# Two chained depthwise convolutions with group norms on one core: pair transfers, windowed band tables, reordered engines, and one more crossed half taken by VectorE

## The chip, the cores and the metric

One core of a Trainium2 chip. The metric is the device time of one execution in microseconds, as a median over several runs; the profile is of one execution, and its span runs from the first to the last instruction.

## The reference

The input x has the shape 4 x 96 x 128 x 128 in float32. Cut to what matters:

```python
def _gn(v, G=32, eps=1e-05):          # mean and variance over 3 channels x 128 x 128
    ...
def _L0_conv_ref(x, w1, w3, w5, alpha):      # depthwise: one 5x5, one 3x3 and one 1x1 kernel per channel
    return alpha[0] * x + alpha[1] * out1 + alpha[2] * out3 + alpha[3] * out5
def _L1_conv_ref(x, w, b):                   # one 3x3 kernel and one bias for all channels
    ...
x = x + _L0_conv_ref(_gn(x), ...)
x = x + _L1_conv_ref(_gn(x), ...)
```

The four terms of the first convolution are one 5x5 kernel per channel. Each channel of each image is convolved by itself, and a group norm needs the whole group of three channels before the first value can be normalized.

## The kernel before

A **unit** is two groups of three channels, for all four images: 16 units (`NU`). Group 0 lies on partitions 0 to 63, group 1 on 64 to 127; a partition holds row p and row 64 + p of an image, its two **halves**. The residual tile `xt` has a ring of six units (`NX`). X is the first convolution, Y the second, and c is a channel of a unit (0 to 2).

TensorE convolves with 64x64 band matrices: the vertical taps are the band, the horizontal taps are shifts of the 512 moving columns (four images of 128). The normalized input is split into a high and a low float16 part (`gn_hi`, `gn_lo`), and the band too, so a channel takes 15 products of four matmuls in X (60) and 9 of four in Y (36). `edge` adds four matmuls with the rows that lie on the other half of the image, from `halo`. Half 0 lands on its own partitions in PSUM; half 1 lands on the other group's partitions and is called **crossed**.

The stages of a unit, by engine:

- VectorE: `x_stats`, eight statistics instructions; `deviations` (L575) and `affine` (L590), which turn the statistics into one scale and one offset for each image; `evacuate` (L617), which adds PSUM times a scale to `xt`: for each X channel three instructions (128 partitions, and two of 64 for the crossed half), for a Y channel one; `y_stats`, eight more.
- TensorE: `mean_product` and `var_product` (two small products over partitions, for the X part of one unit and the Y part of the unit two before it together), then the convolutions.
- ScalarE: `root` (a square root inside `affine`), `normalize` (for each image one full-precision copy into `gn_f` and one float16 copy into `gn_hi`), `cross_over` (L495), which moves the crossed half of each Y channel from PSUM to `cross`.
- GpSimd: `low_part` (L802), `gn_f` minus `gn_hi`; `cross_add` (L814), which adds `cross` to `xt`; `flip_next`, which turns a loaded band round.
- SyncE issues nearly all DMAs, in one order written by hand: loads and stores of units (two DMAs for each image), the band (two), and three steps for each halo: `edges_out` to DRAM, `edges_spread` in DRAM, `edges_in` back. Each step waits for the one before it.

The order on every engine is written by hand in **periods**: period i convolves X of unit i and Y of unit i - 2 (`LAG`). X and Y share the six PSUM banks of `ps`, one for each channel and half, so a convolution waits for the evacuation of the channel before it. The small tiles `mean`, `dev` and `r0` lie in a PSUM bank of their own, `ps_t`.

## Time and profile before

| what | us |
|---|---|
| median of the runs | 478.0 (477.63 to 478.91) |
| the profiled execution's own time | 481.88 |
| its span | 480.1 |
| VectorE busy | 341.8 (71%) |
| TensorE busy | 328.6 (68%) |
| ScalarE busy | 305.1 (64%) |
| GpSimd busy | 274.5 (57%) |
| mean granted TensorE clock | 0.884 of full |

No engine is busy all the time; the periods repeat, so what one period costs is read from the distance between the same event in two periods. The profile counts L12 as line 12 of the kernel.

### The profile page before, as it was taken

Reading aid. Unit: us, or ns where it says so; the run is one execution under the profiler, and the core shown is the slowest. Engines: PE = TensorE matmul, PEld = TensorE weight load, DVE = VectorE, ACT = ScalarE, POOL = GpSimd, SP = SyncE. Lnnn points to the kernel's source line nnn. Section 1 sums busy time; section 2 is a strip of 40 time slices with the busy share of each in tenths; the row PEclk is TensorE's granted clock in tenths of the full one; section 3 lists DMA queues with packets and bytes.
Section 4 is the critical chain, followed back from the end, with each engine's and each line's share of the span. In section 5 each row is a group of like instructions: output and inputs, shape, how many; then the busy total and the mean of one; then the engine's idle time right before and its main releaser. Section 6 shows DMA issues by size and latency. Waiting matters only on the chain.

```text
span 480.1 us, 12659 instructions
## 1 busy us (share of the span) xinstructions
PE 328.6 (68%) x5176; PEld 270.3 (56%) x5176; DVE 341.8 (71%) x740; ACT 305.1 (64%) x373; POOL 274.5 (57%) x196
## 2 busy tenths in 40 slices
PE   2055093987678867879695979758958796965740
PEld 2044093977547745656574666637846585952520
DVE  7396977769787677958595768777687957586510
ACT  0133284778785867685878778784877867828421
POOL 3041455657674766575767657673776766627512
PEclk9999576999979978988989798979999999996975
DMA  8955354635867485848567674768384616150554
GB/s 183 226 120 149 93 138 133 137 106 143 199 184 196 128 197 147 213 138 219 146 189 192 180 201 136 196 196 204 101 218 138 161 59 168 37 148 2 151 145 135
DMA packets 116178, 73.82 MB, mean 154 GB/s; under 512 B 6903, under 2 KB 111479, under 8 KB 116120
## 3 DMA queue, kind: packets, MB, share of 16 engines
q1 hardware_dynamic: 109496, 69.86, 55.2%
q10 hardware_dynamic: 6624, 3.15, 2.9%
q8 instruction: 41, 0.67, 0.6%
q14 instruction: 17, 0.14, 0.1%
HBM read 46.35 MB, written 31.89 MB: 163 GB/s over the span
## 4 chain that ended last, share of the span: by engine, by line
PE 23%; DVE 22%; SPq 17%; DMA 15%; ACT 10%; issue 6%; POOL 3%; ACTq 1%; POOLq 0%; DVEq 0%
PE ps L335 22%; DVE stats L570 10%; DVE xt L625 8%; SPq L242 8%; DMA tap_scratch<-edge_scratch 5%; ACT cross L501 4%; ACT gn_fY L491 3%; DMA haloX<-tap_scratch 3%; ACT gnY L492 3%; POOL gnY L809 3%; DMA edge_scratch<-gnX 2%; SPq L236 2%; SPq L218 2%; SPq L194 2%; DMA haloY<-tap_scratch 1%
## 5 line engine op out<-in xcount | busy, mean ns | idle before, releaser
L335 PE MATMUL ps<-gnX,band 64*64 64x512 f16 x2880 | 191.1, 412 | 12.3 <-ACT gnX L492 12.3
L625 DVE SCALAR_TENSOR_TENSOR xt<-ps,unscale,xt 128x512 f32<-128x512 f32 (+1 forms) x192 | 142.2, 747 | 61.8 <-PE ps L335 60.0
L335 PEld LDWEIGHTS ps<-gnX,band 64*64 64x64 f16 x2880 | 158.6, 190 | 35.9 <-issue 27.0
L809 POOL TENSOR_TENSOR gnX<-gn_fX,gnX 128x768 f16<-128x768 f32 x60 | 92.6, 1543 | 62.1 <-ACT gnX L492 62.1
L570 DVE BATCH_NORM_STATS2 stats<-xt 128x6 f32<-128x384 f32 x256 | 122.4, 546 | 2.4 <-DMA xt<-in_x_dram 1.4
L335 PE MATMUL ps<-gnY,band 64*64 64x512 f16 x1728 | 116.5, 414 | 10.8 <-ACT gnY L492 5.6
L501 ACT ACTIVATE cross<-ps,unscale 64x512 f32<-64x512 f32 x96 | 65.5, 682 | 82.5 <-PE ps L335 81.3
L809 POOL TENSOR_TENSOR gnY<-gn_fY,gnY 128x768 f16<-128x768 f32 x60 | 92.6, 1543 | 33.7 <-ACT gnY L492 33.7
L335 PEld LDWEIGHTS ps<-gnY,band 64*64 64x64 f16 x1728 | 92.6, 190 | 25.3 <-ACT gnY L492 6.2
L818 POOL TENSOR_TENSOR xt<-xt,cross 128x512 f32<-128x512 f32 x48 | 61.2, 1275 | 78.5 <-ACT cross L501 77.4
L491 ACT ACTIVATE gn_fX<-xt,g_add,g_mul 128x768 f32<-128x768 f32 x60 | 61.0, 1017 | 27.6 <-DVE g_add L614 27.6
L492 ACT ACTIVATE gnY<-xt,g_add,g_mul 128x768 f16<-128x768 f32 x64 | 64.6, 1015 | 2.0 <-DVE g_add L614 2.0
L492 ACT ACTIVATE gnX<-xt,g_add,g_mul 128x768 f16<-128x768 f32 x64 | 64.7, 1015 | 1.3 <-DVE g_add L614 1.3
L491 ACT ACTIVATE gn_fY<-xt,g_add,g_mul 128x768 f32<-128x768 f32 x60 | 61.2, 1020 | 2.7 <-DVE g_add L614 2.0
L389 PE MATMUL ps_s<-stats,ones_mean 64*64 64x32 f32 x72 | 6.1, 244 | 60.8 <-DVE stats L570 60.8
L389 PEld LDWEIGHTS ps_s<-stats,ones_mean 64*64 64x64 f32 x72 | 4.6, 150 | 67.0 <-issue 57.6
L335 PE MATMUL ps<-haloX,halo_wX 60*64 60x512 f16 x192 | 21.6, 402 | 30.2 <-DMA haloX<-tap_scratch 30.0
L335 PE MATMUL ps<-haloY,halo_wY 35*64 35x512 f16 x192 | 22.5, 426 | 18.8 <-DMA haloY<-tap_scratch 18.7
L598 DVE RECIPROCAL ps_t<-std 128x8 f32<-128x8 f32 x18 | 3.8, 211 | 41.9 <-ACT std L473 41.9
L335 PEld LDWEIGHTS ps<-haloX,halo_wX 60*64 60x64 f16 x192 | 6.7, 106 | 35.6 <-DMA haloX<-tap_scratch 34.8
L473 ACT ACTIVATE std<-var,eps_t 128x8 f32<-128x8 f32 x18 | 5.2, 288 | 28.7 <-DVE var L594 28.7
L335 PEld LDWEIGHTS ps<-haloY,halo_wY 35*64 35x64 f16 x192 | 9.7, 116 | 23.0 <-DMA haloY<-tap_scratch 22.0
(82 smaller groups left out, 136.6 us busy)
## 6 DMA issues: line engine op xcount, KB each, us to landing
out_dram<-xt SPq DMA_DIRECT2D x124, 192.0 KB, 3.0
xt<-in_x_dram SPq DMA_DIRECT2D x116, 192.0 KB, 3.9
band_raw<-diag_scratch SPq DMA_DIRECT2D x32, 240.0 KB, 3.9
tap_scratch<-edge_scratch SPq DMA_DIRECT2D x16, 246.9 KB, 3.3
haloX<-tap_scratch SPq DMA_DIRECT2D x32, 123.4 KB
xt<-in_x_dram ACTq DMA_DIRECT2D x12, 192.0 KB, 6.3
haloX<-tap_scratch SPq DMA_DIRECT2D x32, 61.7 KB
tap_scratch<-edge_scratch SPq DMA_DIRECT2D x16, 74.1 KB
```

What stands on the lines that cost most here:

```text
L194: eng.dma_start(edge_dram[s][p, :, :, side, 0, :], bass.AP(src.tensor, src.offset, [[R * pitch, 2], [2 * ROW, 2], [1, ROW]]))\
L218: eng.dma_start(halo[s][R * g:R * g + 2 * n, p, :, :, :].rearrange("r b c w -> r (b c w)")[:, 0:EDGE], tap_dram[s][p, g, :, :, 0:EDGE].rea ...
L242: eng.dma_start(out[b, c:c + CG, :, :].rearrange("c (e p) w -> p (c e) w", e=2), xt[HALVES[g], n % NX, b, :, :, :].rearrange("p c e w -> p ...
L335: mm = nc.tensor.matmul(ps[to, c, half, :], weights(rows, half), moving(rows, half), start=first, stop=last)
L389: nc.tensor.matmul(ps_s[rows, 0:8 * NB], ones_mean[rows, :], stats[rows, :, :, :, :].rearrange("h s b e (d t) -> h (s b e d) t", d=2)[:, : ...
L491: nc.scalar.activation(gn_f[s][:, k % NF, :, :, :], src, ACT.Identity, **by)
L492: nc.scalar.activation(gn_hi[s][:, i % 2, :, b, :, PAD:PAD + W].rearrange("p e c w -> p c e w"), src, ACT.Identity, **by).then_inc(hi_done ...
L501: cr = nc.scalar.activation(cross[to, c, :, :].rearrange("p b w -> p (b w)"), ps[frm, c, 1, :], ACT.Identity, scale=unscale[frm, NU * CG:N ...
L570: st = nc.vector.bn_stats(stats[:, at, b, e, :], flat[:, SUB * e:SUB * (e + 1)])
L625: ev = nc.vector.scalar_tensor_tensor(out=here, in0=ps[frm, c, half, :].rearrange("h (b w) -> h b w", b=NB), scalar=unscale[rows, at:at + ...
L809: nc.gpsimd.tensor_tensor(gn_lo[s][:, i % 2, :, b, :, PAD:PAD + W].rearrange("p e c w -> p c e w"), gn_f[s][:, k % NF, :, :, :], gn_hi[s][ ...
L818: nc.gpsimd.tensor_tensor(here, here, cross[:, c, :, :], ALU.add).then_inc(cross_added, 1)
```

## The change

- Channels are assigned to units in pairs: the two units of a pair lie next to each other in DRAM and in `xt`, and one DMA for each image and group of partitions loads or stores both (384 KB instead of 192). Odd periods load a pair, even periods store one. `xt` holds four pairs (eight units). The first two units are still loaded, and the last two stored, one by one.
- The band is written to DRAM in reversed order, as eight overlapping windows for each channel, and is read straight into `band5` by three DMAs of 128 partitions. The turning copies (`flip`) of VectorE and GpSimd go.
- `gn_f` has two slots for each convolution instead of four. The statistics tile has two slots instead of one. `mean`, `dev` and `r0` move from PSUM to SBUF.
- `affine` has six VectorE instructions instead of eight, `deviations` three instead of four: the two `tensor_scalar` instructions (L596, L605) are folded into `scalar_tensor_tensor`.
- New orders: `mean_product` and `var_product` of the statistics that period i - 1 ended with are issued inside the products of X channel 0 of period i, `deviations` moves behind them, and the evacuations of Y channels 1 and 2 move into the next period of VectorE.
- `cross_over` and `cross_add` do channels 0 and 1 only (`NCROSS`); VectorE evacuates both halves of Y channel 2.

```diff
-    NX = 6
-    NF = 4
+    NX = 4
+    NF = 2
+    NCROSS = 2
...
+        def load_pair(eng, m, b):
             for g in range(2):
-                c = 2 * CG * n + CG * g
...
+                c = first_channel(2 * m, g)
+                eng.dma_start(xt[HALVES[g], m % NX, b, :, :, :, :].rearrange("p u c e w -> p (u c e) w"),
+                              x[b, c:c + 2 * CG, :, :].rearrange("c (e p) w -> p (c e) w", e=2)).then_inc(x_in[m % NX], 16)
...
+                for c in range(CG):
+                    k = 4 * CG * (i // 2) + 2 * (CG * (i % 2) + c)
+                    win = diag_dram[k:k + 1, :, :]
+                    sp.dma_start(band5[:, i % 2, c, :],
+                                 bass.AP(win.tensor, win.offset + (R // WIN - 1) * NM,
+                                         [[RUN, 2 * WIN], [-NM, R // WIN], [1, R * NM]])).then_inc(band_in[i % 2], 16)
...
+                    if statistics is not None and n == 5:
+                        mean_product(statistics)
+                    if statistics is not None and n == 12:
+                        var_product(statistics)
...
-                nc.vector.tensor_scalar(var_eps[:, :], var[:, :], GN_EPS, None, ALU.add).then_inc(var_read, 1)
...
+                nc.vector.scalar_tensor_tensor(out=newton[:, :], in0=var[:, :], scalar=GN_EPS, in1=r0[:, :],
+                                               op0=ALU.add, op1=ALU.mult).then_inc(norm_step, 1)
...
-                for rows, half in ((slice(0, P), 0), (LO, 1), (HI, 1))[0:3 if s == X else 1]:
+                for rows, half in ((slice(0, P), 0), (LO, 1), (HI, 1))[0:1 if s == Y and c < NCROSS else 3]:
...
+            for i in range(PERIODS):
+                if i > LAG:
+                    evacuate(Y, i - LAG - 1, 1)
+                    evacuate(Y, i - LAG - 1, 2)
+                if 1 <= i <= NU:
+                    deviations(i + 1)
+                    if i + 2 < NU:
+                        x_stats(i + 2, 0)
+                        x_stats(i + 2, 1)
+                    affine(i + 1)
+                    if i + 2 < NU:
+                        x_stats(i + 2, 2)
+                        x_stats(i + 2, 3)
```

VectorE before, in a steady period, from `y_stats` (the eight statistics) on; `xt<-ps` is an evacuation:

```order
L570 BN_STATS stats<-xt 128x6 x8
L625 SCALAR_TENSOR_TENSOR xt<-ps,unscale,xt 128x4x128
L578 TENSOR_REDUCE ps_t<-ps_s 128x8
L583 TENSOR_TENSOR ps_t<-stats,ps_t 128x32
L585 TENSOR_TENSOR stats<-stats,ps_t 128x32
L587 SCALAR_TENSOR_TENSOR stats<-ps_t,stats 128x32
L625 SCALAR_TENSOR_TENSOR xt<-ps,unscale,xt 128x4x128 x2
L594 TENSOR_REDUCE var<-ps_s 128x8
L596 TENSOR_SCALAR var_eps<-var 128x8
```

and after, from the same `y_stats` on:

```order
L603 BN_STATS stats<-xt 128x6 x8
L651 SCALAR_TENSOR_TENSOR xt<-ps,unscale,xt 128x4x128 x2
L651 SCALAR_TENSOR_TENSOR xt<-ps,unscale,xt 64x4x128 x2
L610 TENSOR_REDUCE mean<-ps_s 128x8
L615 TENSOR_TENSOR dev<-stats,mean 128x32
L617 SCALAR_TENSOR_TENSOR stats<-dev 128x32
L603 BN_STATS stats<-xt 128x6 x4
L624 TENSOR_REDUCE var<-ps_s 128x8
L626 RECIPROCAL r0<-std 128x8
L628 SCALAR_TENSOR_TENSOR newton<-var,r0 128x8
L631 SCALAR_TENSOR_TENSOR newton<-newton,r0 128x8
```

Y channel 0 is now evacuated ahead of the statistics and channels 1 and 2 behind them; two instructions of 64 partitions are added; four X statistics stand between `deviations` and `affine`; and the operands that were named `ps_t` are now SBUF tiles.

TensorE before, from X channel 2 of one period to X channel 0 of the next (`stats,ones_mean` is `mean_product`, `stats,ones_var` is `var_product`):

```order
L335 MATMUL ps<-gnX,band 64x512 x60
L335 MATMUL ps<-haloX,halo_wX 64x512 x4
L335 MATMUL ps<-gnY,band 64x512 x72
L335 MATMUL ps<-haloY,halo_wY 64x512 x4
L389 MATMUL ps_s<-stats,ones_mean 64x32 x2
L335 MATMUL ps<-gnY,band 64x512 x36
L335 MATMUL ps<-haloY,halo_wY 64x512 x4
L396 MATMUL ps_s<-stats,ones_var 64x96 x2
L335 MATMUL ps<-haloY,halo_wY 64x512 x4
```

and after, from X channel 0 of one period to its end:

```order
L363 MATMUL ps<-gnX,band5 64x512 x20
L425 MATMUL ps_s<-stats,ones_mean 64x32 x2
L363 MATMUL ps<-gnX,band5 64x512 x28
L432 MATMUL ps_s<-stats,ones_var 64x96 x2
L363 MATMUL ps<-gnX,band5 64x512 x72
L363 MATMUL ps<-haloX,halo_wX 64x512 x8
L363 MATMUL ps<-gnX,band5 64x512 x60
L363 MATMUL ps<-haloX,halo_wX 64x512 x4
L363 MATMUL ps<-gnY,band3 64x512 x72
L363 MATMUL ps<-haloY,halo_wY 64x512 x4
L363 MATMUL ps<-gnY,band3 64x512 x36
L363 MATMUL ps<-haloY,halo_wY 64x512 x8
```

The products of the statistics have moved out of the Y convolution into the next period's first X channel, and the first use of the X halo stands behind two channels instead of one.

SyncE's queue after, in an even period, from the X halo on (the sizes are rows by pieces):

```order
L288 DMA band<-diag_scratch 128x1x640 x3
L202 DMA edge_scratch<-gnY 4x1x1584 x2
L253 DMA out_dram<-xt 64x12x128 x2
L214 DMA tap_scratch<-edge_scratch 24x1x1580
L253 DMA out_dram<-xt 64x12x128 x4
L226 DMA haloY<-tap_scratch 12x1580
```

Of the stores of a pair, two DMAs stand ahead of the Y halo's second step and four ahead of its third.

## Rows read from the trace of the kernel before

**Rows 1.** The page: span, busy time by engine, and SyncE's DMA queue.

```profile
span 480.1 us, 12659 instructions
...
PE 328.6 (68%) x5176; PEld 270.3 (56%) x5176; DVE 341.8 (71%) x740; ACT 305.1 (64%) x373; POOL 274.5 (57%) x196
...
q1 hardware_dynamic: 109496, 69.86, 55.2%
```

**Rows 2.** Waits: engine, line, released by what: us in total, times, longest.

```profile
PE ps_s L389 <- DVE stats L570: 60.8, 15, 15.0
...
DVE ps_t L598 <- ACT std L473: 41.9, 18, 3.4
...
PE ps L335 <- DMA haloX<-tap_scratch: 30.0, 11, 5.6
...
PE ps L335 <- DMA haloY<-tap_scratch: 18.7, 7, 6.1
```

**Rows 3.** The chain that ended last, at the same place in two periods.

```profile
223.17 0.75 DVE xt L625
...
326.58 0.75 DVE xt L625
```

**Rows 4.** The tile ps by form: durations, first and last start.

```profile
L335 PE MATMUL ps<-haloY,halo_wY x192: 373/377/632, 97.8 to 466.5; 35*64 35x512 f16 x192
```

**Rows 5.** The timeline: the edge matmuls of Y channel 0 of unit 13.

```profile
428.88 0.41 PE L335 MATMUL ps<-haloY,halo_wY 35*64 35x512 f16 x4 [3.63 <-DMA haloY<-tap_scratch]
```

**Rows 6.** Groups of instructions: busy us, mean ns, idle before them.

```profile
L625 DVE SCALAR_TENSOR_TENSOR xt<-ps,unscale,xt 128x512 f32<-128x512 f32 (+1 forms) x192 | 142.2, 747 | 61.8 <-PE ps L335 60.0
...
L809 POOL TENSOR_TENSOR gnX<-gn_fX,gnX 128x768 f16<-128x768 f32 x60 | 92.6, 1543 | 62.1 <-ACT gnX L492 62.1
...
L501 ACT ACTIVATE cross<-ps,unscale 64x512 f32<-64x512 f32 x96 | 65.5, 682 | 82.5 <-PE ps L335 81.3
...
L225 POOL COPY band<-band_raw 128x960 int32<-128x960 int32 x15 | 17.0, 1134 | 0.0
L596 DVE TENSOR_SCALAR var_eps<-var 128x8 f32<-128x8 f32 x18 | 12.8, 711 | 0.6
L605 DVE TENSOR_SCALAR newton<-newton 128x8 f32<-128x8 f32 x18 | 12.6, 699 | 0.6
...
L646 DVE TENSOR_TENSOR gnX<-gn_fX,gnX 128x768 f16<-128x768 f32 x2 | 4.1, 2072 | 0.0
```

**Rows 7.** The timeline of one steady period: start, us, what, count.

```profile
328.90 3.78 DVE L570 BATCH_NORM_STATS2 stats<-xt 128x6 f32<-128x384 f32 x8
...
340.03 3.46 PE L335 MATMUL ps<-gnX,band 64*64 64x512 f16 x60
...
342.91 1.03 ACT L491 ACTIVATE gn_fX<-xt,g_add,g_mul 128x768 f32<-128x768 f32 x1 [1.96 <-DVE g_add L614]
...
347.32 2.64 SPq L242 DMA_DIRECT2D out_dram<-xt  x4
...
349.37 1.01 ACT L492 ACTIVATE gnX<-xt,g_add,g_mul 128x768 f16<-128x768 f32 x1
```

**Rows 8.** The timeline around `affine`, near 412 us.

```profile
411.61 1.54 POOL L809 TENSOR_TENSOR gnY<-gn_fY,gnY 128x768 f16<-128x768 f32 x1 [0.23 <-ACT gnY L492]
...
411.95 1.23 DVE L596 TENSOR_SCALAR var_eps<-var 128x8 f32<-128x8 f32 x1
413.12 2.59 POOL L818 TENSOR_TENSOR xt<-xt,cross 128x512 f32<-128x512 f32 x2
```

**Rows 9.** TensorE in stretches of 2 us: busy, count, granted clock, DMA share, GB/s.

```profile
288.00:290.00 2.00, 0.82 (x16) 1.00 0.03 9
290.00:292.00 2.00, 2.00 (x28) 0.57 0.02 6
```

**Rows 10.** The timeline: `affine` of unit 1, first and last instruction.

```profile
42.03 0.22 DVE L594 TENSOR_REDUCE var<-ps_s 128x8 f32<-128x64 f32 x1 [2.62 <-PE ps_s L396]
...
43.67 0.17 DVE L614 SCALAR_TENSOR_TENSOR g_add<-ps_t,g_mul 128x8 f32<-128x8 f32 x1
```

390 lines of the change are left out of this document (187 added, 203 removed).

## The prediction, made blind

> **What bounds the kernel now.** I read first the busy shares: VectorE 71%, TensorE 68% [rows 1]. Nobody is full, so order and waits set the time. Next the length of a period: the same evacuation stands at 223.17 and 326.58 in the chain, four periods apart [rows 3], 25.85 us each. Between the first edge matmuls of Y channel 0 (unit 0, 97.8 [rows 4]) and those of unit 13 (428.88 [rows 5]) lie 13 periods of 25.5 us. After these 51.2 us are left.
>
> Then the waits [rows 2]. TensorE stands in the middle of Y for the last `y_stats`, 60.8 us in 15 waits, 4 us a period, since `mean_product` is behind Y channel 1 in its queue. VectorE stands 41.9 us, up to 3.4 a time, between `var` and the root: ScalarE is still in `cross_over` and `normalize`. Halos cost TensorE 30.0 and 18.7 us. Inside `affine`, the two `tensor_scalar` (L596, L605) take 711 and 699 ns [rows 6], where an equally small neighbour takes 170 [rows 10]. At 411.95 L596 takes 1.23 us and ends 0.03 us after the GpSimd instruction that had been running [rows 8]: it waits for GpSimd.
>
> VectorE's work of a period is 16 statistics of 0.48 (3.78 for 8 [rows 7]), 12 evacuations of 0.75 [rows 6], and 12 small ones: 7.6 + 9.0 + some 3.7 = 20.3 of 25.5 us. The rest of the period is waiting, and this is what a new order can win.
>
> **The change part by part.** VectorE loses L596 and L605 (1.41 us) and L585 (0.2), and gains two evacuations of 64 partitions, 0.75 each [rows 6]; these take the same time as those of 128, as the mean over both forms shows. The sum is nothing. Sums of busy time: 7.6 + 14 x 0.76 + 9 x 0.22 = 20.2 us.
>
> ScalarE loses two `cross_over` instructions, 2 x 0.68 = 1.4 us a period; GpSimd loses the copy of the band (1.13) and one `cross_add` (1.3, from 2.59 for two [rows 8]). ScalarE then has 16 instructions of 0.92 (from 342.91 to 349.37 are seven steps [rows 7]), four of 0.68 and a root: 17.8 us. GpSimd has 8 x 1.54 + 2 x 1.3 = 14.9 us. These reliefs are worth nothing by themselves; they make room for a period under 25 us, and they leave ScalarE idle when the root comes, so the wait of up to 3.4 us goes.
>
> The new period, laid out by hand from a = 0, the end of the edge matmuls of Y channel 0. VectorE: evacuate Y0 to 0.9 (with 0.15 of signal), `y_stats` to 4.7, Y1 and Y2 (four evacuations) to 7.8, `deviations` 0.7 to 8.5, four X statistics to 10.4, `affine` to 12.1 (it takes 1.81 from 42.03 to 43.84 [rows 10] with eight instructions, so 1.6 with six), four statistics to 14.0, nine X evacuations to 20.9. TensorE: the rest of Y to 2.6, then X channel 0 (60 matmuls in 3.46 [rows 7]). It reaches `var_product` at 6.8 and must wait for `deviations` until 8.5. Then 0.4 for the product, 0.7 for the last twelve matmuls, 3.5 and two edges to 13.6, channel 2 to 17.3, Y0, Y1 and the edge 4.4 to **21.7**, the next a. So TensorE's chain through `deviations` is just ahead of VectorE's own 20.9. The old wait for `y_stats` is now mostly hidden behind five products of X, and what is late next is `deviations`.
>
> The other engines in this layout. ScalarE starts at `affine`'s end A = 12.1: X to A + 7.4, Y0 and Y1 to 11.1, `cross_over` 12.5, Y2 and Y3 16.2, `cross_over` 17.6; then it is idle until the next root. TensorE needs the first `cross_over` at its next X channel 0, at 24.3 to 24.6; it is there at 24.6. `gn_f` with two slots asks that GpSimd (1.54) keeps up with ScalarE's pair (1.84): it does, by 0.3 us, so I cost it at nothing; without that cover each image would cost the difference. GpSimd is through at A + 19.
>
> Transfers: the queue moved 69.86 MB at 55.2% of 480 us [rows 1], 263 GB/s when busy, 4.4 MB a period, 16.6 us of 22 to 23. The X halo starts at A + 9 and is used one channel later than before, some 14 us on; the three steps take about 10. The Y halo has less: `edges_out` about 8 us after a, then 0.77 MB, the spread, 1.54 MB, and the third step. At 263 GB/s these 2.4 MB are 9 us, so it lands at 19 to 20 of 21.7; if a DMA of a pair takes SyncE twice the 0.66 us that one takes now [rows 7], at 21 to 22. I take the halos as hidden, with 1 to 2 us of slack. The band has half a period to spare.
>
> Two prices are not in this layout. First, the **new small instructions with both inputs in SBUF** (two in `deviations`, four in `affine`). The trace of before has only one such form beside GpSimd, L646, with 2.07 us for 768 elements [rows 6]; a statistics of 384 takes 0.48 [rows 7], so some 1 us of it is extra. Below: nothing. Above: each waits one GpSimd instruction, 1.54. But while ScalarE idles, GpSimd runs dry at A + 19; the two in `deviations` come at A + 17.4 to 17.7, in its last `cross_add`, and the four in `affine` behind it. So the pair costs at most 1.3 us; I take 0.6.
>
> The Trainium skill (SBUF — State Buffer, "Who interferes with whom") says that an instruction with two SBUF inputs fully blocks against a GpSimd instruction that reads SBUF, and that one with at most one does not; that speaks against moving `mean`, `dev` and `r0` out of PSUM. By that rule the pair would cost its 1.3 us. The trace agrees for `tensor_scalar` (1.23 us in rows 8), but shows no small two-input case.
>
> Second, **TensorE's clock**. Its pause at `var_product` is 1.7 to 3 us long. In the trace the pause of 2.1 us around 288 (0.82 us busy of 2) is followed by a granted clock of 0.57, near the 1.2 GHz level [rows 9]; X channel 0 at full clock takes 3.46. Most pauses of this length left the clock alone, those of 3.5 us and more did not. A dip costs about 1.7 us; between none and one a period, I take one in three: 0.6.
>
> The period: 21.7 + 0.6 + 0.6 = **22.9**, with ends at 21.7 and 21.7 + 1.3 + 1.7 = 24.7.
>
> **Opening and end.** Before, the first `affine` waits behind the band's turning, and the second ends at 43.84 [rows 10], behind the constants. After, it comes directly behind them, about 8 us sooner, and periods 1 and 2 save 1 us each: Y channel 0 of unit 0 at 87.8 instead of 97.8. The end I leave at 51.2: the last `affine` no longer waits some 3 us for its root, but the second halo step of unit 15 now stands in SyncE's queue behind a store that waits for unit 14's evacuations, which I put at the same 3 us.
>
> Sum: 87.8 + 13 x 22.9 + 51.2 = 436.7 us of span. The profiled execution took 481.88 against a span of 480.1, the median is 478.0, so the median lies 2.1 below the span: **434.6**.
>
> **The rivals.**
> 1. *The halos are late.* For it: SyncE's queue is one, the pairs put 1.5 MB in one piece ahead of the Y halo, and halos cost 49 us before [rows 2]. Against it: the first use comes later, and half as many loads and stores are issued. If the Y halo is 2 us late every period: 24.9, or 87.8 + 323.7 + 51.2 - 2.1 = 461. Chance 0.18.
> 2. *Nothing of the two prices comes.* Period 21.7: 87.8 + 282.1 + 51.2 - 2.1 = 419 us. Chance 0.17.
> 3. *Slower: the small instructions line up behind GpSimd.* If ScalarE does not run dry before `affine`, because another wait shifts it, GpSimd starts its next instruction in each of the 0.04 us between two small ones, and all six wait up to 1.54: 9.2 us. On VectorE's own 20.9 this is 30.1 a period, and 87.8 + 391.3 + 51.2 - 2.1 = 528. Against it: GpSimd is busy 14.9 of 22.9 us only. It decides from where the six waits are over 5.4 us a period (26.3 = 25.5 + 10 / 13). Chance 0.04. The rule of the Trainium skill named above is the one that it would take.
> 4. *The order gains nothing*, since a loop through ScalarE (A to A + 17.6, root, `affine`) or the pair transfers keep the period near 25. ScalarE's loop is 19.6, so little speaks for it; opening alone: 468 to 478. Chance 0.05.
>
> The forecast itself has 0.56. The range reaches down to 417 and up to 454, within which the forecast, rival 2 and the mild half of rival 1 lie. The forecast's own range is 424 to 446. A measurement of this kernel tells apart 0.3%, 1.4 us. Faster 0.94, same 0.02, slower 0.04.
>
> **What would show it.** In the profile after: the distance of two periods 22.9; no wait of VectorE for the root over 0.5 us; TensorE's wait for `y_stats` under 1 us and a new one, 1.7 to 3 us, ahead of `var_product` (L432); ScalarE's busy sum near 283, GpSimd's near 237, VectorE's as before; L615 and L617 longer than 0.2 us, those of `affine` near 0.17. Mean granted clock 0.93 or more. The prediction is wrong if `haloY` waits stand in every period, if L628 to L641 take over 0.5 us each, or if the clock falls behind each `var_product`.

## The result, and the profile after

The changed kernel takes **458.22 us** (median of four runs, 456.87 to 459.14) where the kernel before took 478.46 in the same session: ratio 0.957, interval 0.954 to 0.960. Forecast were 434.6 us and a range of 417 to 454. The direction was right, the gain (20.2 us) was a little under half of the 43.4 forecast, and the time lies outside the range. Some executions of a kernel are disturbed and longer: the ratios here leave them out, while the times are medians over all executions (with such executions two of e12's four, one of e11's four and one of e14's ten).

The page after: span, busy time by engine, and the chain that ended last, by engine (compare [rows 1]; SPq is SyncE's queue).

```profile
span 455.0 us, 12402 instructions
...
PE 319.9 (70%) x5176; PEld 275.4 (61%) x5176; DVE 340.8 (75%) x716; ACT 283.2 (62%) x341; POOL 237.4 (52%) x165
...
SPq 26%; DVE 23%; DMA 21%; PE 11%; ACT 10%; issue 4%; POOL 3%; DVEq 0%
```

The busy sums are the forecast ones: ScalarE 283, GpSimd 237, VectorE as before. The chain shows what the layout did not expect: 47% of it are SyncE's queue and DMAs. The waits after (engine, line, released by what: us, times, longest), for [rows 2]:

```profile
PE ps L363 <- DMA haloY<-tap_scratch: 36.8, 13, 6.9
PE ps_s L432 <- DVE stats L617: 34.1, 15, 3.5
PE ps_s L425 <- DVE stats L603: 31.4, 11, 10.1
PE ps L363 <- DMA haloX<-tap_scratch: 9.3, 1, 9.3
```

TensorE's wait for `y_stats` has halved (60.8 before), and its last 31.4 us include one of 10.1 in the opening. The new wait ahead of `var_product` (L432) is 2.3 us a time, as forecast. The wait for the X halo fell from 30.0 to 9.3, one wait in the opening. That for the Y halo has not gone away but doubled, 18.7 to 36.8, and stands in 13 of the 16 units; waits in every period were the prediction's own sign of being wrong. VectorE's small instructions (busy, mean ns | idle before), for [rows 6]:

```profile
L615 DVE TENSOR_TENSOR dev<-stats,mean 128x32 f32<-128x32 f32 x18 | 10.7, 593 | 0.6
...
L617 DVE SCALAR_TENSOR_TENSOR stats<-dev 128x32 f32<-128x32 f32 x18 | 4.6, 257 | 0.6
...
L626 DVE RECIPROCAL r<-std 128x8 f32<-128x8 f32 x18 | 3.7, 203 | 8.4 <-ACT std L508 8.4
...
L628 DVE SCALAR_TENSOR_TENSOR newton<-var,r 128x8 f32<-128x8 f32 x18 | 3.0, 167 | 0.6
```

The wait for the root fell from 41.9 to 8.4 us; `affine`'s instructions take 0.17 to 0.20 us each; only the pair in `deviations` is long, 0.45 us together above two times 0.20. The mean granted clock is 0.909, where 0.93 or more was forecast (0.884 before).

The edge matmuls of Y, by the tile's view, and those of channel 0 of units 13 to 15, by the timeline, for [rows 4, 5]:

```profile
L363 PE MATMUL ps<-haloY,halo_wY x192: 373/376/633, 96.2 to 443.0; 35*64 35x512 f16 x192
```

```profile
400.76 0.51 PE L363 MATMUL ps<-haloY,halo_wY 35*64 35x512 f16 x4
...
422.30 0.64 PE L363 MATMUL ps<-haloY,halo_wY 35*64 35x512 f16 x4 [6.49 <-DMA haloY<-tap_scratch]
...
438.26 0.64 PE L363 MATMUL ps<-haloY,halo_wY 35*64 35x512 f16 x4 [6.92 <-DMA haloY<-tap_scratch]
```

So the three terms of the sum came out as follows: opening 96.2 (forecast 87.8), period (400.76 - 96.2) / 13 = 23.43 (22.9), end 455.0 - 400.8 = 54.2 (51.2). The misses are 8.4, 6.9 and 3.0 us, 18.3 together. The other 5.3 of the 23.6 us lie in the step from span to median: the forecast put the median 2.1 us below the profiled span, and it lies 3.2 above (458.2 against 455.0).

SyncE's queue in an even period, in which the edge matmuls of Y channel 0 come at 262.9 and then at 285.1:

```profile
271.14 1.09 SPq L202 DMA_DIRECT2D edge_scratch<-gnY  x2
272.33 1.35 SPq L253 DMA_DIRECT2D out_dram<-xt  x2
274.24 0.84 SPq L214 DMA_DIRECT2D tap_scratch<-edge_scratch  x1
275.18 4.93 SPq L253 DMA_DIRECT2D out_dram<-xt  x4
280.22 1.43 SPq L226 DMA_DIRECT2D haloY<-tap_scratch  x1
281.69 1.30 SPq L228 DMA_DIRECT2D haloY<-tap_scratch  x1
283.03 0.29 SPq L226 DMA_DIRECT2D haloY<-tap_scratch  x1
```

Each of the four stores ahead of the third step holds SyncE 1.23 us, and even the first small DMAs behind them take 1.4 us where 0.3 is usual. The halo is there at 285.1, 22 us after the last one: the case that the prediction gave as "at 21 to 22" and set aside.

This is the mild half of the periods. In the odd ones, which load, the halo comes later. The third step of the period before, and the edge matmuls at the end of both:

```profile
255.90 1.59 SPq L226 DMA_DIRECT2D haloY<-tap_scratch  x1
...
258.21 0.29 SPq L228 DMA_DIRECT2D haloY<-tap_scratch  x1
```

```profile
262.93 0.51 PE L363 MATMUL ps<-haloY,halo_wY 35*64 35x512 f16 x4 [2.90 <-DMA haloY<-tap_scratch]
...
285.14 0.41 PE L363 MATMUL ps<-haloY,halo_wY 35*64 35x512 f16 x4 [0.92 <-DMA haloY<-tap_scratch]
```

In the even period TensorE goes on 1.5 us after the last small DMA was issued, in the odd one 4.4 us after it, though SyncE had issued it by 19.3 us after the edge matmuls before (20.2 in the even one). So it is in the periods of units 1 to 10: 1.5 to 2.7 us behind stores, 3.9 to 4.8 behind loads, and TensorE waits 0.9 to 1.8 us in the even and 2.0 to 3.9 in the odd ones. What SyncE's queue does not explain there is the landing itself, behind loads that take 5.8 us (median) to land; e13 comes back to this.

### The profile page after: what moved, and what is told of

It reads as the page before. It is cut to its first block, busy times and chain, and to the rows that moved or that the text cites. A ratio compares the mean times of both kernels' runs of the same rounds, so it can differ in the third digit from the quotient of the medians.

```text
span 455.0 us, 12402 instructions
## 1 busy us (share of the span) xinstructions
PE 319.9 (70%) x5176; PEld 275.4 (61%) x5176; DVE 340.8 (75%) x716; ACT 283.2 (62%) x341; POOL 237.4 (52%) x165
## 4 chain that ended last, share of the span: by engine, by line
SPq 26%; DVE 23%; DMA 21%; PE 11%; ACT 10%; issue 4%; POOL 3%; DVEq 0%
PE ps L363 11%; DVE stats L603 10%; DVE xt L651 10%; SPq L253 8%; DMA tap_scratch<-edge_scratch 6%; ACT gnX L528 5%; ACT gn_f L527 4%; DMA edge_scratch<-gnX 4%; DMA haloY<-tap_scratch 4%; SPq L226 4%; DMA edge_scratch<-gnY 3%; SPq L228 3%; SPq L288 3%; DMA diag_scratch<-diag 3%; SPq L240 2%
## 5 line engine op out<-in xcount | busy, mean ns | idle before, releaser
L651 DVE SCALAR_TENSOR_TENSOR xt<-ps,unscale,xt 64x512 f32<-64x512 f32 (+1 forms) x224 | 166.2, 748 | 73.4 <-PE ps L363 70.5
L363 PE MATMUL ps<-gnX,band 64*64 64x512 f16 x2880 | 186.9, 398 | 9.3 <-ACT gnX L528 6.5
L834 POOL TENSOR_TENSOR gnX<-gn_f,gnX 128x768 f16<-128x768 f32 x60 | 92.6, 1544 | 120.3 <-ACT gnX L528 120.3
L527 ACT ACTIVATE gn_f<-xt,g_add,g_mul 128x768 f32<-128x768 f32 x120 | 122.1, 1017 | 17.5 <-DVE g_add L641 17.2
L834 POOL TENSOR_TENSOR gnY<-gn_f,gnY 128x768 f16<-128x768 f32 x60 | 92.6, 1544 | 27.1 <-ACT gnY L528 25.5
L363 PEld LDWEIGHTS ps<-gnY,band 64*64 64x64 f16 x1728 | 96.3, 190 | 13.4 <-issue 10.4
L537 ACT ACTIVATE cross<-ps,unscale 64x512 f32<-64x512 f32 x64 | 43.7, 682 | 41.6 <-PE ps L363 40.6
L843 POOL TENSOR_TENSOR xt<-xt,cross 128x512 f32<-128x512 f32 x32 | 40.7, 1272 | 39.7 <-ACT cross L537 39.7
L363 PE MATMUL ps<-haloY,halo_wY 35*64 35x512 f16 x192 | 19.3, 426 | 36.8 <-DMA haloY<-tap_scratch 36.8
L432 PE MATMUL ps_s<-stats,ones_var 64*64 64x96 f32 x72 | 7.7, 296 | 34.1 <-DVE stats L617 34.1
L432 PEld LDWEIGHTS ps_s<-stats,ones_var 64*64 64x64 f32 x72 | 4.5, 151 | 40.4 <-DVE stats L617 39.6
L425 PE MATMUL ps_s<-stats,ones_mean 64*64 64x32 f32 x72 | 5.8, 237 | 31.4 <-DVE stats L603 31.4
L363 PEld LDWEIGHTS ps<-haloX,halo_wX 60*64 60x64 f16 x192 | 10.3, 108 | 10.3 <-DMA haloX<-tap_scratch 9.7
```

What stands on the lines that cost most here:

```text
L363: mm = nc.tensor.matmul(ps[to, c, half, :], weights(rows, half), moving(rows, half), start=first, stop=last)
L527: nc.scalar.activation(gn_f[:, f_slot(s, i, b), :, :, :], src, ACT.Identity, **by)
L537: cr = nc.scalar.activation(cross[to, c, :, :].rearrange("p b w -> p (b w)"), ps[frm, c, 1, :], ACT.Identity, scale=unscale[frm, NU * CG:N ...
L651: ev = nc.vector.scalar_tensor_tensor(out=here, in0=ps[frm, c, half, :].rearrange("h (b w) -> h b w", b=NB), scalar=unscale[rows, at:at + ...
L834: nc.gpsimd.tensor_tensor(gn_lo[s][:, i % 2, :, b, :, PAD:PAD + W].rearrange("p e c w -> p c e w"), gn_f[:, f_slot(s, i, b), :, :, :], gn_ ...
L843: nc.gpsimd.tensor_tensor(here, here, cross[:, c, :, :], ALU.add).then_inc(cross_added, 1)
```

## The experiments

Three theories of the lost time stood against each other. **A**: transfers in SyncE's one queue hold up the halos, in the opening, in the periods and at the end. **B**: the operands that moved into SBUF make VectorE wait for GpSimd, and TensorE with it. **C**: the loop through the engines is that long by itself. The table has each run's time, and from its profile the first edge matmuls of Y channel 0 of unit 0, the mean period from there to unit 13, what is left behind that, and TensorE's waits for the two halos (us).

| kernel | time | ratio to before (interval) | unit 0 | period | end | haloY | haloX |
|---|---|---|---|---|---|---|---|
| after | 458.22 | 0.957 (0.954 to 0.960) | 96.2 | 23.43 | 54.2 | 36.8 | 9.3 |
| e1_halo_first | 451.57 | 0.945 (0.938 to 0.951) | 95.4 | 23.53 | 47.6 | 25.8 | 9.2 |
| e2_opening_units | 452.08 | 0.945 (0.939 to 0.951) | 89.4 | 23.56 | 53.9 | 35.6 | 2.2 |
| e3_psum | 456.41 | 0.954 (0.947 to 0.960) | 95.9 | 23.31 | 54.7 | 43.9 | 9.3 |
| e4_three_crossed | 462.13 | 0.965 (0.958 to 0.972) | 97.6 | 23.54 | 58.4 | 45.3 | 9.6 |
| e5_tail | 455.0 | 0.953 (0.946 to 0.959) | 94.4 | 23.63 | 49.6 | 32.8 | 8.4 |
| e6_all | 441.58 | 0.920 (0.915 to 0.925) | 88.9 | 23.25 | 50.6 | 34.8 | 5.5 |
| e7_units | 446.32 | 0.930 (0.926 to 0.934) | 88.7 | 23.64 | 46.7 | 34.9 | 2.2 |
| e8_act_stores | 494.53 | 1.029 (1.026 to 1.032) | 95.3 | 26.26 | 52.9 | 49.1 | 9.3 |
| e9_no_stores | 442.23 | 0.921 (0.918 to 0.925) | 96.0 | 22.88 | 47.6 | 10.6 | 8.0 |
| e10_bare | 440.02 | 0.921 (0.914 to 0.928) | 94.4 | 22.74 | 45.9 | 8.6 | 8.1 |
| e12_units_all | 441.44 | 0.917 (0.904 to 0.931) | 88.9 | 23.53 | 43.9 | 37.3 | 2.0 |
| e13_act_halo | 491.34 | 1.024 (1.019 to 1.030) | 96.1 | 26.10 | 53.4 | 50.1 | 10.3 |
| e14_all_act_halo | 479.24 | 0.998 (0.995 to 1.002) | 88.5 | 26.16 | 49.2 | 58.1 | 1.2 |
| e15_bare_psum | 417.13 | 0.868 (0.864 to 0.873) | 96.8 | 21.02 | 46.3 | 9.1 | 7.6 |
| e16_units_act_halo | 460.93 | 0.961 (0.956 to 0.965) | 89.0 | 25.01 | 44.9 | 29.8 | 4.9 |
| e17_units_order | 440.89 | 0.919 (0.912 to 0.927) | 89.5 | 23.44 | 44.6 | 28.5 | 10.3 |
| e18_units_behind | 462.5 | 0.965 (0.959 to 0.970) | 90.5 | 25.07 | 44.4 | 7.8 | 36.0 |

### The edits one by one

**e1_halo_first**: image 2 behind the third step.

```diff
-                in_and_out(j, (1, 2))
+                in_and_out(j, (1,))
                 if y >= 0:
                     edges_in(sp, Y, y)
+                in_and_out(j, (2,))
```

> The changed kernel with one edit: of each pair, the two DMAs of image 2 are issued behind the third step of the Y halo instead of ahead of it. Theory A (the period is 23.4 us instead of the 22.9 that was forecast because the pair's DMAs of images 1 and 2, 1.54 MB, stand ahead of the Y halo's last step): TensorE's waits for haloY, 36.8 us in the changed kernel, of which some 23 lie in the steady periods, fall below 8 us there, and the time falls by 5 to 12 us, from 458 to about 449. Rival B (the period is set by VectorE's chain, deviations waiting for GpSimd): the waits move to another place and the time stays within 2 us of 458.

It gained 6.6 us, all of it in the end; the period is what it was. The expectation on the period failed: the image that no longer delays the Y halo delays the X halo, the band and the next Y spread. In the period shown above the third step of the X halo starts at 270.2 instead of 267.8 and the next Y spread at 276.5 instead of 274.2, so that the next third step of Y starts at 280.6, where it started at 280.2.

**e2_opening_units**: pair 1 in single units, unit 2 first.

```diff
-            for b in range(NB):
-                load_pair(sp, 1, b)
+            for b in range(NB):
+                load_unit(sp, 2, b, x_pair1_in[0])
...
+                    if j == 0:
+                        load_unit(sp, 3, b, x_pair1_in[1])
```

> The changed kernel with one edit: the second pair (units 2 and 3) is loaded as two single units, unit 2 where the pair was loaded, unit 3 behind the first X halo, in period 0. Theory A (the opening was forecast 8 us too short because eight DMAs of 384 KB stand ahead of the X halo of unit 0 and because the statistics of unit 2 wait for the whole pair): edge matmuls of X unit 0 start at 42 to 44 instead of 48.9 us, Y channel 0 of unit 0 ends 4 to 6 us sooner than 96.2, and the time falls by 4 to 6 us, to about 453. Rival B (the opening is bound by the reads of the band table behind its own 1.1 MB of writes, or by VectorE): less than 2 us.

The time (452.08) is theory A's. Unit 0 comes 6.8 us sooner, at 89.4, 1.6 from the forecast's 87.8. SyncE's queue of the changed kernel, in the opening:

```profile
26.21 10.38 SPq L240 DMA_DIRECT2D xt<-in_x_dram  x8
36.73 1.35 SPq L198 DMA_DIRECT2D edge_scratch<-gnX  x4
42.03 0.59 SPq L214 DMA_DIRECT2D tap_scratch<-edge_scratch  x1
```

and of e2:

```profile
25.91 5.33 SPq L235 DMA_DIRECT2D xt<-in_x_dram  x8
31.46 1.21 SPq L199 DMA_DIRECT2D edge_scratch<-gnX  x4
35.82 0.58 SPq L215 DMA_DIRECT2D tap_scratch<-edge_scratch  x1
```

Eight DMAs of twice the size take SyncE twice as long, and the X halo of unit 0 starts 5.3 us later. TensorE's 9.3 us for haloX become 2.2.

**e3_psum**: `mean`, `dev` and `r0` in PSUM again, with the fourth instruction in `deviations` that this needs.

```diff
-        mean = sb("mean", [P, 2 * NB])
+        mean = ps_t[:, 0:2 * NB]
...
+                nc.vector.tensor_tensor(halves, halves, mean_of, ALU.subtract).then_inc(norm_step, 1)
```

> The changed kernel with the three small tiles mean, dev and r0 back in PSUM, and with the four-instruction form of deviations that this needs (one small instruction of 0.24 us more a period). Theory A (the wait for GpSimd comes from the two SBUF inputs, and is some 0.3 to 1.0 us a period on the way to var_product): L615 falls from up to 1.27 us to 0.20, TensorE's wait for var_product shrinks by the same, and the time changes by -6 to +1 us, likeliest -3. Rival B (halo waits take up what is won): within 1 us, either way.

The median is 1.8 us lower, less than the intervals can tell apart. The waits are rival B's: TensorE's wait ahead of `var_product` fell from 34.1 to 27.0 us, and its wait for haloY rose from 36.8 to 43.9: the halo takes what the lock gives back, 7.1 us each.

**e4_three_crossed** undoes the edit that the change is named for; the third `cross_over` and `cross_add` stand directly behind the second.

```diff
-    NCROSS = 2
+    NCROSS = 3
```

> The changed kernel with NCROSS 3: ScalarE moves and GpSimd adds the crossed half of Y channel 2 again, VectorE evicts only its first half. Theory A (forecast: VectorE's two more evacuations of 0.75 us stand on the way to deviations, since they are in front of it, while ScalarE and GpSimd have room): VectorE gets to deviations 1.5 us sooner, GpSimd is then busy 1.3 us longer just when deviations comes, TensorE's wait for var_product falls by 0 to 1.5 us a period, and the time lies between 0 and 10 us lower. Rival B (ScalarE's loop then reaches 19.2 us plus root and GpSimd's last cross_add delays the stores and with them the Y halo): 2 to 10 us slower.

The median is 3.9 us higher, as rival B had it, but its interval (0.958 to 0.972) touches that of the changed kernel (0.954 to 0.960). In the profile 4.2 us stand in the end; the period moves by 0.1. The two instructions of `deviations` in e4:

```profile
L618 DVE SCALAR_TENSOR_TENSOR stats<-dev 128x32 f32<-128x32 f32 x18 | 17.9, 992 | 0.6
L616 DVE TENSOR_TENSOR dev<-stats,mean 128x32 f32<-128x32 f32 x18 | 15.8, 875 | 0.6
```

With the third `cross_add`, GpSimd works on while `deviations` runs, and the pair costs 1.47 us more than its 0.4 instead of 0.45. TensorE's wait ahead of `var_product` fell all the same, from 34.1 to 25.9 us, and that for haloY rose from 36.8 to 45.3: the same trade as in e3, 8.2 against 8.5 us.

**e5_tail**: in the last two periods the halo steps go ahead of the stores.

```diff
-                in_and_out(j, (0,))
+                if j < NU:
+                    in_and_out(j, (0,))
...
-                in_and_out(j, (3,))
+                in_and_out(j, (3,) if j < NU else range(NB))
```

> One edit: in the last two periods SyncE issues the halo steps of Y first and the stores behind them; all else is as in the changed kernel. Theory A, that the end of 54.2 us (before 51.2) is long because the second and third step of the Y halo stand behind store DMAs: the end falls to 48 us or so, 458.2 - 6 = 452 us, with the first 13 periods unchanged at 23.4 us. Rival B, that the stores put off to the end of the program have to be waited for there: 457 to 461 us. Rival C, that the gain of e1_halo_first at the end came from the order in periods 14 and 15, which this edit touches not at all: 456 to 458 us.

The end fell by 4.6 us in the profile, less than the 6 of theory A. The time fell by 3.2, but its interval (0.946 to 0.959) holds the 0.957 of the changed kernel, so the time alone does not show it.

**e6_all**: e1, e2, e3 and e5 in one.

> Four edits at once: one image ahead of the third step of the Y halo (alone it took 6.6 us off), pair 1 loaded as single units with unit 2 first (alone 6.1 us off), mean, dev and r0 in PSUM (alone 1.8 us off), and in the last two periods the steps of the halo ahead of the stores. Theory A, that each took its time off a place of its own (end, opening, steady periods): 458.2 - 6.6 - 6.1 - 1.8 = 443.7 us, with another 0 to 2 us off for the stores of the last two periods: 442 to 444. Rival B, that the steady periods are held by the loop of the Y halo, so that what PSUM gives back turns into a longer wait for haloY: 444 to 446 us, with a period of 23.4 us as before. Rival C, that the first and second edit use the same slack: 447 to 451 us.

By the time the gains of e1, e2 and e3 add up (14.5 us, with 0 to 2 more for e5's edit; 16.6 measured). By the profile theory A holds for the opening only (7.3 us): 2.3 lie in the periods and 3.6 in the end, where e1 alone had 6.6 and e5 alone 4.6.

**e7_units**: single units in every period, at the same places of the queue.

```diff
-                    if j % 2 and 2 <= m < NU // 2:
...
-                        load_pair(sp, m, b)
+                    elif n < NU:
...
+                        load_unit(sp, n, b, x_in[n // 2 % NX])
+                    if j >= 3:
+                        unit_ready(j - 3)
+                        store_unit(sp, j - 3, b)
```

> The joint transfers are undone and nothing else: every period loads one unit and stores one unit with DMAs of 192 KB at the queue places where the DMAs of 384 KB stood, the opening as in e2_opening_units. Theory A, that a pair's DMA of 384 KB, which holds SyncE for 1.2 to 1.3 us where one of 192 KB took 0.66 us, and the burst of eight of them in one period delay the Y halo: the wait for haloY in the steady periods falls by half, the period from 23.4 to about 22.9 us, so 452.1 - 13 x 0.5 = 445 us. Rival B, that only the bytes count, which stay the same: the period stays 23.4 us and the time that of e2_opening_units, 452 us. Rival C, that sixteen DMAs of half the size in every period cost SyncE more, since now the odd periods have stores and the even ones loads too: 456 to 462 us.

The time is the one theory A gave, the reason is not: the period stayed (23.64), the 5.8 us against e2 are more than accounted for by the end (53.9 to 46.7). As many bytes stand in front of the halo, and SyncE takes as long for them: in e12, which has the same transfers, 5.2 us for four loads and four stores of 192 KB, where the changed kernel has 4.93 for four of 384. What the joint form costs lies in the end; that a pair waits there for its second unit I only argue from the code.

**e8_act_stores**: the stores of pairs 0 to 6 from ScalarE's queue.

```diff
-                        store_pair(sp, m, b)
...
+                if j % 2 == 0 and j // 2 >= LAG:
...
+                    for b in range(NB):
+                        store_pair(act, m, b)
```

> The stores of pairs 0 to 6 are issued by ScalarE behind its last copy of the period, so that SyncE's queue holds only halo steps, bands and loads. Theory A, that SyncE's one in-order queue delays the Y halo behind stores: the third step of the Y halo comes 3 to 5 us sooner in even periods, the wait for haloY falls from 36.8 us to under 20, the period from 23.43 to 22.7 us, and the end by about 5 us as in e1_halo_first: 458.2 - 13 x 0.7 - 5 = 444 us. Rival B, that a DMA of 384 KB holds ScalarE's queue as long as it held SyncE (8 x 1.2 = 10 us in every second period), so that the next normalization is late: the period rises to 24 us or more and the time to 460 to 470 us. Rival C, that the transfers are bound by the 16 DMA engines whichever queue issues them: the halo stays late, 455 to 459 us.

Rival B, and more of it. ScalarE in e8:

```profile
205.67 7.32 ACTq L253 DMA_DIRECT2D out_dram<-xt  x4
213.03 0.30 ACT L505 ACTIVATE std<-var,eps_t 128x8 f32<-128x8 f32 x1 [7.16 <-issue]
```

The root stands behind the stores; periods with stores take 35 us, the others 21.2.

**e9_no_stores** leaves out the stores of pairs 0 to 6; a load into their place waits for the evacuations instead of the store.

```diff
-                        store_pair(sp, m, b)
+                        pass
```

> The stores of pairs 0 to 6 are left out (only the last two units of the output are written); all else stays. This is the bound of what the stores can cost. Theory A, that the stores in SyncE's queue set the length of the even periods: the period falls to 22.5 to 22.9 us, the end by 5 to 6 us, so 458.2 - 13 x 0.7 - 5.5 = 443.5 us, and an even period is no longer than an odd one. Rival B, that the engines' own loop of two periods (affine, normalization, low part, three steps of the Y halo, edge matmuls) sets the period whatever the queue does: the period stays at 23.2 to 23.5 us and only the end falls, 451 to 453 us. Rival C, that the loads and the band, which stay, hold the queue in the odd periods: 447 to 450 us, with the gain in the even periods alone.

The periods now alternate between 20.9 and 25 us. Busy time and transfers of one with loads and one without:

```profile
233.40:258.20 24.80, 18.38 (x326) 16.87 (x318) 21.14 (x39) 20.13 (x24) 16.63 (x12) 1.00 0.67 154
258.20:279.10 20.90, 19.27 (x320) 16.91 (x324) 19.53 (x39) 15.78 (x20) 13.05 (x10) 0.92 0.39 105
```

(us from and to, length, TensorE, weight loads, VectorE, ScalarE, GpSimd, granted clock, DMA share, GB/s.) In the long one SyncE issues four loads ahead of the third step (4.71 us from 246.16) and the halo lands at 258.2; in the short one the third step starts 2.6 us behind the spread. The time is theory A's, the pattern rival C's: the gain lies in the even periods. But TensorE's wait for haloY in that long period is 1.87 us, and it also stands 3.48 us ahead of `var_product`, so the loads alone do not make it long.

**e10_bare** also leaves out the loads of pairs 4 to 7; units 8 to 15 work on what lies in SBUF.

```diff
-                    if j % 2 and 2 <= m < NU // 2:
+                    if j % 2 and 2 <= m < NX:
```

> The stores of pairs 0 to 6 and the loads of pairs 4 to 7 are left out (units 8 to 15 work on what lies in SBUF from the units before, and only the last two units of the output are written). From period 4 on SyncE's queue then holds nothing but halo steps and bands. Theory A, that bulk transfers in the one in-order queue hold the Y halo in every second period at least: without them every period is like the short ones of e9_no_stores, 20.9 us, no wait for haloY over 1 us is left, and with the end of about 47.5 us the time is 96.2 + 3 x 23.4 + 10 x 20.9 + 47.5 - 0 = 423 us. Rival B, that the loop of two periods over affine, normalization, low part and the three halo steps is the bound even with an empty queue: 22.6 us a period at the least, 437 to 440 us. Rival C, that VectorE with TensorE's clock at 0.92 to 1.00 is the bound: 21.5 to 22 us a period, 429 to 434 us.

Theory A's 423 us failed: 440.0, within rival B's numbers but not for its reason. No haloY wait is left in the steady periods, and still they are 21.2, 24.1 and 23.0 us in turn, 22.73 on average from unit 5 to 13. One of the long ones, around `deviations`:

```profile
215.87 1.54 POOL L835 TENSOR_TENSOR gnY<-gn_f,gnY 128x768 f16<-128x768 f32 x1 [0.23 <-ACT gnY L526]
...
216.29 1.17 DVE L613 TENSOR_TENSOR dev<-stats,mean 128x32 f32<-128x32 f32 x1
217.37 1.26 POOL L844 TENSOR_TENSOR xt<-xt,cross 128x512 f32<-128x512 f32 x1
217.50 1.20 DVE L615 SCALAR_TENSOR_TENSOR stats<-dev 128x32 f32<-128x32 f32 x1
...
218.75 0.43 PE L430 MATMUL ps_s<-stats,ones_var 64*64 64x96 f32 x2 [3.49 <-DVE stats L615]
```

Both instructions end within 0.1 us of the GpSimd instruction that ran when they started (217.41 and 218.63). TensorE pauses 3.49 us, and its granted clock behind the pause is at the 1.2 GHz level (length, busy, clock, DMA share, GB/s):

```profile
216.00:218.00 2.00, 0.00 (x0) 1.00 0.59 180
218.00:220.00 2.00, 1.25 (x16) 0.65 0.69 227
220.00:222.00 2.00, 2.00 (x24) 0.50 0.01 3
222.00:224.00 2.00, 2.00 (x42) 1.00 0.15 42
```

Both longer kinds of period hold such a stretch: the 24.1 us behind a pause of 3.5 us, the 23.0 (from 232.3 to 255.3, for one) behind one of 2.1 to 2.2. The 21.2 us hold none.

**e15_bare_psum**: e10 with e3's edit.

> e10_bare (no stores of pairs 0 to 6, no loads of pairs 4 to 7) with mean, dev and r0 in PSUM and the deviations in four instructions. Theory A, that without transfers the deviations' wait of up to 3.5 us and the lower clock behind it make the difference between periods of 21.2 and 24.1 us: the mean period falls from 22.7 to 22.0 us or less, 440.0 - 10 x 0.7 = 433 us. Rival B, that the lock hides behind ScalarE's chain of affine and normalization: 438 to 440 us.

The bare kernel falls from 440.0 to 417.1 us, more than theory A asked for. Every steady period is now 20.8 us, with the clock at 1.00:

```profile
245.30:266.10 20.80, 18.11 (x328) 17.00 (x324) 19.28 (x40) 17.98 (x22) 14.85 (x11) 1.00 0.24 69
```

The small instructions and the product that waits for them:

```profile
253.59 0.20 DVE L616 TENSOR_TENSOR stats<-stats,ps_t 128x32 f32<-128x32 f32 x1
253.83 0.20 DVE L618 SCALAR_TENSOR_TENSOR stats<-ps_t,stats 128x32 f32<-128x32 f32 x1
...
254.09 0.30 PE L431 MATMUL ps_s<-stats,ones_var 64*64 64x96 f32 x2 [1.64 <-DVE stats L618]
```

With one operand in PSUM the pair takes 0.40 us (0.60 with the extra instruction of this form), though a GpSimd instruction runs beside it (1.54 from 253.06). e10 and e15 together are the small two-input case that the trace before did not show.

The Trainium skill (SBUF — State Buffer, "Who interferes with whom") says that a VectorE instruction with two SBUF inputs contends with a GpSimd instruction that reads SBUF, and that one with at most one does not, outside the modes that use both ports. The traces agree with both halves: 1.17 and 1.20 us in e10, 0.20 each in e15.

Together with e3 and e10 this excludes theory C and shows that A and B each describe one of two waits: with both removed the loop runs at 20.8 us.

**e13_act_halo**: only the third step of the Y halo goes to ScalarE, between images 1 and 2 of its X normalization.

```diff
-                    edges_in(sp, Y, y)
...
+                    normalize(X, j + 1, j + 1, 0, (0, 1))
+                if y >= 0:
+                    edges_in(act, Y, y)
```

> The four DMAs of the third step of the Y halo are issued by ScalarE, between the second and third image of its normalization of X, instead of by SyncE behind images 1 and 2 of the pair; all else is as in the changed kernel. Theory A, that their place in SyncE's in-order queue delays them: they are issued at a + 16 us instead of a + 16.8 and take 0.3 us each instead of 1.4, the halo lands 2 to 3 us sooner in periods with transfers and 4 to 6 us sooner in the end; the period falls to 22.9 us and the time to 458.2 - 13 x 0.5 - 5 = 447 us. Rival B, that the 16 DMA engines are the bottleneck: the halo lands as late as before, and ScalarE, held 1.3 us more, makes it 458 to 461 us. Rival C, that SyncE, freed of the halo, now issues the second pair of transfers sooner and the spread and bands of the next period stand behind them: 450 to 455 us.

All three theories failed in size. SyncE, ScalarE and TensorE in one period:

```profile
275.00 0.72 SPq L214 DMA_DIRECT2D tap_scratch<-edge_scratch  x1
275.76 5.37 SPq L240 DMA_DIRECT2D xt<-in_x_dram  x4
```

```profile
279.89 0.30 ACTq L226 DMA_DIRECT2D haloY<-tap_scratch  x1
...
281.35 1.03 ACT L525 ACTIVATE gn_f<-xt,g_add,g_mul 128x768 f32<-128x768 f32 x1 [6.06 <-issue]
```

```profile
287.85 0.64 PE L361 MATMUL ps<-haloY,halo_wY 35*64 35x512 f16 x4 [6.53 <-DMA haloY<-tap_scratch]
```

The four small DMAs are issued at 0.3 us each, by 281.2, and land at 287.9, 6.6 us later: no sooner than the loads that SyncE had issued until 281.1 (6.2 us to landing, the median of these loads). Here a queue of its own bought nothing against transfers that were under way, as the odd periods of the changed kernel already suggest (1.3 us of issue in e13 as against 2.6, and 6.6 us to landing as against 4.4). Besides, the spread lands 4.9 us after its issue and ScalarE, in order, stands still for it: the 6.06 us of idle time that delay the normalization and make the period 26 us. The Trainium skill (DMA: Bandwidth & Descriptors, "Queues, rings and completion order") says that a DMA's completion is reported only after all earlier writes of the same DMA engine, whichever queue they came from. By that rule a landing together with the loads is to be expected; the trace agrees with it, but does not tell whether the halo's bytes or only its signal were late.

**e14_all_act_halo** is e13 with the edits of e2, e3 and e5; **e16_units_act_halo** is the same with single units in every period.

> As e13_act_halo, with pair 1 as single units, mean, dev and r0 in PSUM, and the halo steps ahead of the stores in the last two periods. If the three add to e13_act_halo as they did to each other: e13's time less 6 (opening), less 2 (PSUM), less 1 to 3 (end), so 436 to 440 us where e13 is at 447. If the wait for haloY takes up what they free: 441 to 444 us, as e6_all.

> As e14_all_act_halo, with single-unit transfers in every period in place of the joint ones. Theory A, that joint and single transfers are worth the same once the halo is out of SyncE's queue: within 2 us of e14_all_act_halo. Rival B, that single units are better because no period has eight DMAs of 384 KB in its queue: 3 us or more faster than e14. Rival C, that the sixteen DMAs a period of SyncE delay bands and X halo: 3 us or more slower.

The period of 26.1 stays in e14, and its 12.1 us against e13 are opening and end; both of its expectations failed, as e13's did. e16 is 18 us faster than e14, with a period of 25.0: rival B. Every period now has half the loads and half the stores, and TensorE's wait for haloY is half that of e14, 29.8 against 58.1 us; why single units help the period here and not in e7 was not taken further.

**e11_behind** and **e18_units_behind**: images 1 and 2 both behind the third step, once joint, once in single units.

```diff
-                in_and_out(j, (1, 2))
                 if y >= 0:
                     edges_in(sp, Y, y)
+                in_and_out(j, (1, 2))
```

> As e6_all, but images 1 and 2 of the pair both stand behind the third step of the Y halo and ahead of the first step of the next X halo; image 0 stays ahead of the spread and image 3 at the end of the period. Theory A, that the Y halo's lateness sets the period and SyncE is idle for 6 us behind its third step: the third step comes 2 us sooner in every period than in e6_all, the period falls from 23.25 to 22.8 us or less, and the time from 441.6 to 433 to 437 us. Rival B, that the four DMAs push the first step of the X halo 3 to 5 us out, so that haloX is late instead (waits of 2 us or more for haloX in most periods): 441 to 448 us.

> As e12_units_all, with images 1 and 2 both behind the third step of the Y halo, ahead of the first step of the X halo. In joint form (e11_behind, 472.0 us) this cost 30 us through waits for haloX. If the bytes ahead of the X halo are what cost it, they are the same here, and the time is 465 to 475 us. Rival B, that only the burst of a period with a pair hurt, through back-pressure that lasts into the X halo: with even periods 440 to 450 us.

e11 took 472.04 us (ratio 0.985, 0.974 to 0.996), far above both of its expectations, e18 462.5. The rows are e18's. Now the Y halo is early and the X halo late. TensorE in e18:

```profile
PE ps L366 <- DMA haloX<-tap_scratch: 36.0, 11, 5.6
...
PE ps L366 <- DMA haloY<-tap_scratch: 7.8, 5, 4.7
```

The wait for one halo has become that for the other and has grown: 36.0 + 7.8 us, where e12 has 37.3 + 2.0. e18's time lies 2.5 us below the range of its first expectation, and far from its rival.

**e12_units_all** (e7, e3 and e5 in one) and **e17_units_order** (that with e1's edit).

> As e7_units (joint transfers undone), with mean, dev and r0 in PSUM and the halo steps ahead of the stores in the last two periods. Theory A, that the effects add up: 446.3 - 1.8 - 0 to 2 = 443 to 445 us, so no better than e6_all's 441.6 us, which keeps the joint transfers. Rival B, that even spread of the transfers and free operands in PSUM help each other, because no period is long: 436 to 440 us. Rival C, that what PSUM gives back turns into a longer wait for haloY: 445 to 447 us.

> As e12_units_all, with image 2's load and store moved from ahead of the third step of the Y halo to behind it: 0.75 MB instead of 1.5 MB stand between the spread and the gather. If those bytes are what the period pays for, at the 1.23 us that 384 KB took: the gather comes 2.5 us sooner, the wait for haloY falls by half, the period from 23.5 to 22.7 us, and the time to 441.4 - 13 x 0.5 = 435 us. Rival B, as e1_halo_first showed in joint form: the X halo, the bands and the next spread come later by the same, and the period stays: 439 to 443 us.

e6, e12 and e17 lie within 0.7 us of each other, and their intervals overlap: 0.920 (0.915 to 0.925), 0.917 (0.904 to 0.931), 0.919 (0.912 to 0.927). These are the best complete kernels here, some 17 us below the changed one. e12 fell between the numbers of its three theories, and with its interval it decides none of them. In e17 the haloY wait fell from 37.3 to 28.5 and the haloX wait rose from 2.0 to 10.3 (rival B).

## Why the prediction was wrong, step by step

- **The busy sums and what they leave** held: ScalarE 283.2 (283 forecast), GpSimd 237.4 (237), VectorE unchanged; the wait for the root fell to 8.4 us in 18 times.
- **The layout by hand** (21.7 us, VectorE's own chain 20.9) was right and a little long: e15 runs it at 20.8.
- **The price of the operands in SBUF** (0.6 of at most 1.3 a period) is 0.45 in the changed kernel, where the halo's lateness covers it, and, with the pauses and clock that it brings, 22.73 - 20.79 = 1.9 us in the bare kernel. The bound of 1.3 was too low: in e10 both instructions wait, 1.17 + 1.20 - 0.4 = 2.0 us. The agreement with the Trainium skill that the prediction saw for `tensor_scalar` is none for two SBUF inputs: L596 reads one SBUF tile, and its 1.23 us go against "one with at most one does not", to which the prediction had not put the section's exception for the modes that use both ports.
- **The clock** was costed for the pause at `var_product`. In the changed kernel five of the six stretches of lower clock between 96 and 400 us stand behind the halo waits of the odd periods instead (2.0 to 3.9 us; the next 36 matmuls of Y take 3.4 to 3.8 us, 2.2 in the even periods). Behind `var_product` it is one, after a pause of 3.48 us; pauses of 1.7 to 2.6 us there left 70 matmuls at 4.14. So there are six dips in 13 periods, where one in three was taken, and five of them come with the late halo. A dip costs about what was taken (1.7): behind the pause shown above e10's next 70 matmuls of X took 5.53 us, 1.4 over the 4.14 at full clock, and behind others up to 5.80.
- **"I take the halos as hidden, with 1 to 2 us of slack"** is the step that failed in the period. Laid out by bandwidth, 8 + 9 = 17 us pass from a (the end of the edge matmuls) to the third step, and so it was in the periods of units 1 to 10: it starts 16.4 to 18.1 us after a. From there the prediction gave 2 to 3 us to the landing, at 19 to 20. Measured are 2.6 to 3.6 us for issuing its four DMAs, and 1.5 to 2.7 (behind stores) or 3.9 to 4.8 (behind loads) to the landing: 21.7 to 25.3 in all. Without transfers in the steady periods the mean period is 22.74; with them it is 23.43. That is 9 us over 13 periods, more than the whole miss of 6.9 there.
- **That 22.74 lies within 0.2 of the forecast's 22.9 is luck**: the layout was 0.9 too long (21.7 for 20.8) and the two prices 0.7 too low (1.2 for 1.9).
- I also looked only along one period: a late Y halo holds `evacuate(Y, 0)`, which stands ahead of `y_stats` in VectorE's order, hence `affine` and the normalization from which the Y halo after next comes, so that lateness is handed on. This I argue from the order; no run isolates it.
- **The opening** failed by 8.4 us: `affine` of unit 1 ended at 36.5, near the forecast (about 8 us before 43.84), but the change's `load_pair(sp, 1, b)` puts 3.1 MB ahead of the X halo of unit 0, and I had not followed SyncE's queue there. e2 gives 6.8 us back by that alone.
- **The end** failed by 3.0 us: I had the second step of the Y halo behind a store, but not the third one behind four more. e1 gives 6.6 us back, e5 4.6 in its profile.
- **From span to median** 5.3 us were lost: the 2.1 us by which the median lay below the span came from one long profiled execution (481.88, where the runs took 477.63 to 478.91), and I carried them over as if they belonged to the kernel. The profiled execution after is the fastest of its four (456.87), and the median lies 3.2 us above its span.
- **The sum as a sum** failed too. Removing the lock alone moves the period by 0.1 us, the transfers alone by 0.7, both by 2.4. Two waits that can stand for each other have no prices of their own. Rival 1 (late halos, 461 us, chance 0.18) was the right mechanism and deserved the larger chance, since nothing excluded it but an estimate by bandwidth. That its time is only 3 us off is luck: its period of 24.9 is 1.5 too long, 19 us in all, and the opening, the end and the step to the median are 16.7 too short.

Open: why e10's periods go in a cycle of three, what decides whether a pause of 2 to 3.5 us lowers the clock, and whether e13's halo data or only its completion was late. A kernel with e15's period and all its transfers was not found.
